# A tiled mixture-of-experts stage: first weights from memory for each tile, and the sums of seven batches on VectorE

## The reference

```python
# B, T, C = 8, 512, 128; 16 heads of 64; E = 8 experts, K = 2, I = 512
x = layernorm(x + attention(x))                # q, k with rope, causal softmax, out @ Wo + bo
weights = softmax(x @ gate_w.T + expert_bias)
top_w, top_i = top_k(weights, 2)
top_w = top_w / (sum(top_w) + 1e-6)
for e in range(E):
    h = gelu(x @ w_up[e].T)                    # 128 -> 512
    out += sparse_w[..., e] * (h @ w_down[e].T)   # 512 -> 128
out = (out - mean(out)) * rsqrt(var(out) + 1e-5) + x
x = layernorm(x + out)
```

## Time and profile before

| | before |
|---|---|
| three runs, us | 857.59, 857.94, 859.91 (median 857.94) |
| profiled execution, us | 857.98, its span 856.2 |
| PE busy | 809.1 us, 95% of the span |
| VectorE, ScalarE, GpSimd busy | 679.8, 630.8, 560.5 us |
| chain that ended last | PE 88%, DVE 5%, ACT 2%, POOL 2% |
| granted PE clock, mean | 0.984 |
| transfers | 41.43 MB, mean 48 GB/s |

### The profile page before, as it was taken

How to read it: one execution, slowest core, us unless ns; L and a number is a source line. 1 busy time by engine, 2 the same in 40 slices (tenths; PEclk the granted TensorE clock), 3 DMA queues, 4 the chain that set the end, 5 groups by cost and what they waited for, 6 DMA issues and landing times.

```text
span 856.2 us, 20971 instructions
## 1 busy us (share of the span) xinstructions
PE 809.1 (95%) x6238; PEld 582.7 (68%) x6238; DVE 679.8 (79%) x2696; ACT 630.8 (74%) x1674; POOL 560.5 (65%) x587
## 2 busy tenths in 40 slices
PE   7999999999999999999999999999999899999950
PEld 2556666666666666666666666666666599999950
DVE  5777798889888988898888889888988576333695
ACT  3677887888788778877787788777787856556543
POOL 4665656556755665576668665765686178898982
PEclk9999999999999999999999999999999999999985
DMA  5111101001000100010001000100022232322714
GB/s 160 32 39 38 51 20 32 8 23 37 28 26 17 48 17 27 14 51 14 26 14 51 14 28 17 48 14 17 28 60 70 67 91 73 79 76 83 212 65 123
DMA packets 52414, 41.43 MB, mean 48 GB/s; under 512 B 6096, under 2 KB 46160, under 8 KB 52304
## 3 DMA queue, kind: packets, MB, share of 16 engines
q1 hardware_dynamic: 47952, 31.11, 13.2%
q0 software_dynamic: 4352, 8.99, 3.0%
HBM read 23.74 MB, written 12.14 MB: 42 GB/s over the span
## 4 chain that ended last, share of the span: by engine, by line
PE 88%; DVE 5%; ACT 2%; POOL 2%; issue 2%; DMA 0%; POOLq 0%; SPq 0%; DVEq 0%; ACTq 0%
PE TB L864 18%; PE SB L824 17%; PE TB L850 14%; PE AO L885 6%; PE SB L997 6%; PE AO L745 4%; PE SB L850 3%; PE AO L747 3%; PE AO L746 3%; PE AO L1006 3%; PE TB L1006 3%; PE AO L742 1%; PE AO L813 1%; PE AO L815 1%; PE AO L814 1%
## 5 line engine op out<-in xcount | busy, mean ns | idle before, releaser
L1083 ACT ACTIVATE Pr_all<-Sm,nmax 128x512 f32<-128x512 f32 (+3 forms) x512 | 279.6, 550 | 2.3 <-DVE nmax L1259 2.3
L1259 DVE CUSTOM_DVE_ANT_0 Sm<-SB,causal 128x512 f32<-128x512 f32 (+3 forms) x512 | 220.0, 486 | 72.2 <-PE SB L824 72.2
L534 POOL TENSOR_TENSOR shared<-shared,sin_t 128x512 f32<-128x512 f32 x63 | 80.3, 1274 | 187.0 <-DVE shared L1239 187.0
L1095 ACT ACTIVATE PT<-TB 128x1024 f32<-128x1024 f32 (+1 forms) x188 | 133.0, 742 | 65.4 <-PE TB L850 65.4
L824 PE MATMUL SB<-kT,qT 64*128 64x512 f32 (+3 forms) x1024 | 167.0, 444 | 2.4 <-DVE nmax L1259 1.9
L864 PE MATMUL TB<-PT,shared 128*64 128x128 f32 x1008 | 152.1, 441 | 2.4 <-ACT PT L1095 0.5
L1280 DVE SCALAR_TENSOR_TENSOR x_acc<-AO,rinv,x_acc 128x128 f32<-128x128 f32 x504 | 141.7, 344 | 5.1 <-PE AO L885 2.8
L850 PE MATMUL TB<-ident,Pr_all 128*128 128x128 f32 x1008 | 134.7, 277 | 1.6 <-ACT PT L1095 1.6
L850 PEld LDWEIGHTS TB<-ident,Pr_all 128*128 128x128 f32 x1008 | 108.6, 140 | 38.8 <-ACT Pr_all L1083 20.6
L824 PEld LDWEIGHTS SB<-kT,qT 64*128 64x128 f32 x1024 | 78.8, 187 | 72.0 <-issue 52.3
L1083 ACT ACTIVATION_READ_ACCUMULATOR Pr_all<-Sm,nmax 128x1 f32 x512 | 97.1, 190 | 0.0
(11 more groups left out here) (281 smaller groups left out, 1425.7 us busy)
## 6 DMA issues: line engine op xcount, KB each, us to landing
wo<-in_wo SPq DMA_DIRECT2D x64, 64.0 KB, 1.8
PT<-yrows SPq DMA_DIRECT2D x7, 512.0 KB, 4.7
xt<-xrows SPq DMA_DIRECT2D x40, 65.0 KB, 2.1
x_acc<-in_x SPq DMA_DIRECT2D x8, 256.0 KB
wdown<-in_wdown SPq DMA_DIRECT2D x8, 256.0 KB, 3.3
pay<-pay SPq DMA_DIRECT2D x8, 256.0 KB, 2.8
x_acc<-pay SPq DMA_DIRECT2D x8, 256.0 KB, 3.2
shared<-in_wup SPq DMA_DIRECT2D x8, 256.0 KB, 3.0
```

The costliest lines, as they stand in the source:

```text
L534: nc.gpsimd.tensor_tensor(k_rot, k_rot, sin_t[:, :], ALU.mult).then_inc(k_mul, 1)
L1083: nc.scalar.activation(Pr[j][:, 0:n], Sm[j], ACT.Exp, bias=nmax[:, j:j + 1], scale=-1.0, accum_out=rsum[p][:, h * QB + qb:h * QB + qb + 1] ...
L1095: last = nc.scalar.activation(PT[p][:, :, 0:qb + 1, qb * P:qb * P + P], source, ACT.Copy)
L1259: nc.vector.tensor_tensor_reduce(out=Sm[j], in0=SB[2 * (group % 2) + h][:, at:at + n], in1=causal[:, T - n:T], scale=-0.125, scalar=HUGE, ...
```

## The change

First weights are no longer kept on chip: SP loads the 256 KB of the tile's expert from memory into `w_tile[t % 4]`, four steps after the tile's rows (`XLEAD`). VectorE copies nothing between tiles, runs batch 7's routing without waiting for tiles, and then sums and measures batches 0 to 6 in two groups and one (`settle`, `root_front`). GpSimd's sums are gone; its spacers end at tile 66. There are 71 tiles. The batch loads and the pads move: pads to SP's steps 24 to 31, batch loads behind the weights of tiles 56 to 59, 64 and 65. ScalarE's order in the tail follows. The core of the diff:

```diff
-TILES = (B * T * K + E * (P - 1)) // P + 1
-TILES += -TILES % 4
+TILES = (B * T * K + E * (P - 1)) // P
+TABLE = TILES + -TILES % 4
-UP_AT = {58: (4,), 59: (5,), 60: (0, 1), 61: (2, 3), 62: (6, 7)}
-LAST_COPY, LAST_BEFORE = 20, (5, 6, 9, 11)
-LAST_PADS = (25, 26, 27, 28, 29, 30, 31, 32)
-LOAD_AT = {0: 63, 1: 64, 2: 65, 3: 66, 4: 71, 5: 71}
-POOL_SUM_AT = {56: (3, 0), 57: (3, 2), 61: (4, 0), 62: (4, 2), 63: (5, 0), 64: (5, 2)}
-AHEAD = GROUP
+LAST_COPY, LAST_BEFORE = 14, (5, 6, 9, 11)
+LAST_PADS = (24, 25, 26, 27, 28, 29, 30, 31)
+LOAD_AT = {0: 56, 1: 57, 2: 58, 3: 59, 4: 64, 5: 65}
+AHEAD, XLEAD = GROUP, 4
...
         @block.sync
-                if u in UP_AT:
...
-            def load_up(e):
-                sp.dma_start(wup[:, e * I:e * I + I], wup_h[:, e * I:e * I + I]).then_inc(w_in, 16)
...
-            def tile_loads(t, s, first, last):
+            def load_rows(t, s):
...
+            def load_weights(t):
+                if t == 2:
+                    sp.wait_ge(scored, BLK * (UNITS - 1))
+                if t % GROUP == 0:
+                    experts[:] = values(mybir.EngineType.SP, tile_expert, t, GROUP, E - 1)
+                wait(sp, up_done, t - AHEAD + 1)
+                sp.dma_start(w_tile[t % AHEAD][:, :], wup_h[:, bass.ds(experts[t % GROUP] * I, I)]).then_inc(w_tile_in[t % AHEAD], 16)
+            rows, experts = [None] * GROUP, [None] * GROUP
+            for t in range(TILES + XLEAD):
+                if t == EARLY:
+                    last_rows()
+                if t < TILES:
+                    load_rows(t, t % XT)
+                if t >= XLEAD:
+                    load_weights(t - XLEAD)
                 for b, at in LOAD_AT.items():
-                    if t == at:
+                    if t - XLEAD == at:
                         load_y(b)
...
         @block.gpsimd
-                if t in POOL_SUM_AT:
-                    sum_half(*POOL_SUM_AT[t])
-                elif t < TILES - 2:
+                if t < TILES - 4:
                     space()
...
         @block.tensor
-                pe.wait_ge(w_ready, t + 1)
+                pe.wait_ge(w_tile_in[t % AHEAD], 16 * (t // AHEAD + 1))
...
-                    pe.wait_ge(w_in, 16 * 2 * E)
+                    pe.wait_ge(w_in, 16 * E)
...
         @block.scalar
             root_half(0, FRONT)
-            root_sum(FRONT, KNOWN + 1)
             for b in range(FRONT):
                 norm2_of(b, QB - 1, 1)
             root_half(FRONT, KNOWN)
+            for b in range(FRONT, KNOWN):
+                norm2_of(b, QB - 1, 2)
+            root_half(KNOWN, KNOWN + 1)
             root_sum(B - 1, B)
-            norm2_of(FRONT, QB - 1, 2)
-            root_half(KNOWN, KNOWN + 1)
-            norm2_of(FRONT + 1, QB - 1, 2)
...
         @block.vector
-            def take_expert(t, e):
-                wait(dve, up_done, t - AHEAD + 1)
-                nc.vector.tensor_copy(w_tile[t % AHEAD][:, :], wup[:, bass.ds(e * I, I)]).then_inc(w_ready, 1)
...
+            def root_front(first, end):
+                of = slice(QB * first, QB * end)
+                bits, root, old = row_bits[:, 0:QB * (end - first)], rstd2[:, 0, of], root_f[:, 0:QB * (end - first)]
+                dve.wait_ge(var1, end)
...
+                for i in range(NEWTON):
...
-            tiles(dve, ffn)
+            for t in range(LAST_TABLE + 9):
+                route_last(t)
...
+            def settle(first, end):
+                for b in range(first, end):
+                    sum_two(b, b)
+                    stats_sum(b)
+                root_front(first, end)
+                for b in range(first, end):
+                    add_x1(b)
+                    stats_half(b)
+            settle(0, FRONT)
+            settle(FRONT, KNOWN)
+            sum_two(KNOWN, KNOWN)
+            stats_sum(KNOWN)
+            factors(1, 0, FRONT)
+            root_front(KNOWN, KNOWN + 1)
+            factors(2, FRONT, KNOWN)
+            add_x1(KNOWN)
+            stats_half(KNOWN)
+            factors(3, KNOWN, KNOWN + 1)
             sum_last()
-            stats_half(KNOWN)
-            factors(2, FRONT, KNOWN)
-            invert_sum(2, B - 1, B)
+            invert_sum(1, B - 1, B)
             add_x1(B - 1)
-            factors(3, KNOWN, KNOWN + 1)
             stats_half(B - 1)
             factors(4, B - 1, B)
```

More of the change, by code:

```diff
@@ L286, in build_block @@
         up_done, gelu_done = sem("up_done"), sem("gelu_done")
-        w_ready = sem("w_ready")
+        w_tile_in = [sem(f"w_tile_in{i}") for i in range(AHEAD)]
         down_done, y_ready = sem("down_done"), sem("y_ready")
@@ L475, in tile_loads @@
                 sp.dma_start(xt[s], xrows[bass.ds(rows[t % GROUP], P), :]).then_inc(xt_in[s], 16)
+            def load_weights(t):
[13 more added lines that the diff above has]
+                    load_weights(t - XLEAD)
                 for b, at in LOAD_AT.items():
-                    if t == at:
+                    if t - XLEAD == at:
                         load_y(b)
-            rows = [None] * GROUP
-            tiles(sp, tile_loads, last_rows)
             for b in range(KNOWN, B):
@@ L1502, in final_table @@
                 if step == 8:
[L1503 removed]
+                    write_tables(1, route_bank(B - 1), slice(EARLY, TABLE))
             def attention(u, p, n, batch, first, last):
@@ L1606, in route_last @@
                     final_table(t - LAST_TABLE)
-                for b in range(FRONT):
-                    if t == SUM_AT.get(b):
-                        sum_two(b, b)
-                    if t == STATS2_AT[b]:
-                        stats_sum(b)
-                if t == ROOT_AT:
-                    seed_front()
-                if t == ROOT_REST_AT:
-                    refine_front(2)
-                for b in range(FRONT):
-                    if t == ADD_AT[b]:
-                        add_x1(b)
-                    if t == HALF_AT[b]:
-                        stats_half(b)
             def norm_rows(b):
@@ L1650, in refine_front @@
-            def refine_front(n):
-                for i in range(n):
-                    root = rstd2[:, 0, front]
-                    done(nc.vector.tensor_tensor(root_f[:, :], root, root, ALU.mult))
-                    done(nc.vector.scalar_tensor_tensor(out=root_f[:, :], in0=root_f[:, :], scalar=-0.5, in1=sd2[:, 0, front],
-                                                        op0=ALU.mult, op1=ALU.mult))
-                    done(nc.vector.scalar_tensor_tensor(out=root, in0=root_f[:, :], scalar=1.5, in1=root, op0=ALU.add, op1=ALU.mult))
@@ L1659, in ffn @@
-            def ffn(t, s, first, last):
-                if first:
-                    dve.wait_ge(tables_ready, 1)
-                    dve.wait_ge(w_in, 16 * 2 * E)
-                    for ahead, e in enumerate(experts(0, AHEAD)):
-                        take_expert(ahead, e)
-                if t == EARLY - AHEAD:
-                    dve.wait_ge(tables_ready, 2)
-                if t in EXPERTS_AT:
-                    of = EXPERTS_AT[t]
-                    next_experts.extend(experts(of[0], of[1] - of[0]))
-                if t + AHEAD < TILES:
-                    take_expert(t + AHEAD, next_experts[t])
-                route_last(t)
+            def root_front(first, end):
+                of = slice(QB * first, QB * end)
+                bits, root, old = row_bits[:, 0:QB * (end - first)], rstd2[:, 0, of], root_f[:, 0:QB * (end - first)]
+                dve.wait_ge(var1, end)
+                done(nc.vector.tensor_scalar(sd2[:, 0, of], mv2[:, 0, of, 1], 4.0, 4 * LN_EPS, ALU.mult, ALU.add))
+                done(nc.vector.tensor_scalar(bits, sd2[:, 0, of].bitcast(I32), 1, None, ALU.arith_shift_right))
+                done(nc.vector.tensor_scalar(root.bitcast(I32), bits, -1.0, ROOT_SEED, ALU.mult, ALU.add))
+                for i in range(NEWTON):
+                    done(nc.vector.tensor_tensor(old, root, root, ALU.mult))
+                    done(nc.vector.scalar_tensor_tensor(out=old, in0=old, scalar=-0.5, in1=sd2[:, 0, of], op0=ALU.mult, op1=ALU.mult))
+                    done(nc.vector.scalar_tensor_tensor(out=root, in0=old, scalar=1.5, in1=root, op0=ALU.add, op1=ALU.mult))
```

52 lines of the change are left out of this document (3 added, 49 removed).

## The result

The changed kernel takes 864.21 us (median of 5 runs, 863.23 to 865.39) beside 859.91 for the kernel before in the same session (5 runs, 857.59 to 860.78): a ratio of 1.0058, 95% interval 1.0039 to 1.0078. It is slower by 0.6%. The forecast was 859.7 against 857.94; by the ratio the result is 862.9 on that footing (857.94 x 1.0058), inside the range and 3.2 us above the sum.

What follows compares the result with a forecast made beforehand. It took PE, without idle time over the tiles, and then a tail of normalisation to bound the kernel. Terms -1.9 + 5.4 + 2.5 - 4.3 = +1.7 us on 857.94 gave 859.7, range 853.5 to 867.5.

Steps and rivals of the forecast that it cites:

- SP's queue at the pads: At tiles 20, 24 and 28, table reads and pads delay SP's weight loads; PE waits 0.8, 3.3 and 1.3: together 5.4 us.
- The batch loads, 2.5 predicted: After tiles 56 to 59, 512 KB loads make SP's steps 2.05 us: weights 2.3 late, tile 66's 0.2; together 2.5 us.
- Landing: ... 3.2: Each 256 KB weight load lands 3.2 us after issue: 3.0 plus 0.2 for the rows queued ahead.
- 0.4 late within those 2.3: Behind the batch loads, 2.6 us of transfer work in 2.05 us steps makes tile 59's weights 0.4 late, inside the 2.3.
- The tail, -4.3 predicted: From the last result to the last normalisation: 18.5 us in place of 22.8, VectorE later than ScalarE by 0.3.
- one tile fewer, -1.9: On PE's path: 71 tiles instead of 72 save one beat, 1.9 us.
- SP keeps up: Rival: reads overlap or SP's steps are cheaper, stalls are 0, VectorE sets the tail: 852.6 us; chance 0.2, wholly or mostly.
- Landings late everywhere: Rival: weight loads take 5.0 us, eleven groups lose 0.6 each, bad places 1.8 more: +8.4, 868.1 us; chance 0.2.
- PE's clock: Rival: PE's clock falls in longer stalls, each tile after costing up to 1.9 us more; counted within late landings' 0.2.
- a stall of 3.3 us: PE's predicted wait before tile 24; shorter than 4.2 us of idle time, so the clock stays at 2.4 GHz.
- the forecast's own range, 857 to 863: Whole kernel: spread of the main forecast, by table reads of 1.3 or 1.5 us and landings of 2.8 to 3.8.
- line of 0.3%: Whole kernel: smallest difference a measurement can tell, 2.6 us; chances faster 0.22, same 0.41, slower 0.37.

Runs made afterwards that it cites:

- fixed_experts: The changed kernel with SP reading no table of experts, tile t taking expert t modulo 8: 859.7 us, 1.0006 of the kernel before.
- pads_spread: The changed kernel with pads sent at SP's steps 25, 27, 29 to 39 instead of 24 to 31: 865.39 us, 1.0089 of the kernel before.
- deep8: The changed kernel with eight buffers for the first weights instead of four: 861.6 us, 1.0039 of the kernel before.
- pool_reads: The changed kernel with GpSimd adding two SBUF buffers of 448 columns behind each send from tile 58 on: 884.24 us, 1.0271 of the kernel before.
- tiles71: The kernel before with 71 tiles instead of 72, the loads of batches 4 and 5 one step earlier: 857.51 us, 0.9991 of the kernel before.
- deep8_spaced: The changed kernel with eight weight buffers and the loads of batches 0 to 5 three tiles apart: 872.33 us, 1.0134 of the kernel before.
- half_weights: The changed kernel with each tile's weight load bringing 128 KB instead of 256 KB: 864.04 us, 1.0068 of the kernel before.

## Why the prediction came out as it did

*SP's queue at the pads, 5.4 predicted.* Right, 6.1: SP's times to 0.3 us, and the cause (`fixed_experts`, `pads_spread`, `deep8`). At tile 28 PE was 5.1 us behind the kernel before (tile 0's 0.4 taken off), where 5.4 was predicted; part of it had come out early, at tiles 21, 25 and 26, whose loads took 3.9 to 4.7 us and not 3.2. The other 0.9, at tile 29, is a landing of 4.9 and was not predicted.

*The batch loads, 2.5 predicted.* **This is the step that was wrong in size**, 5.9. "Landing: ... 3.2" was taken for every load, alone or behind 512 KB. The transfers' side was in the text: 2.6 us of work in steps of 2.05, and it said "0.4 late within those 2.3". But work that isn't done stays in the queue for the next step, so by the prediction's own figures four steps leave 2.2 us; and if loads are served in order, an estimate, a weight load issued 1.15 us behind a batch load that takes 4.7 alone can't land before 3.6 us. Measured, from the issue of the weights of tiles 57 and 58 on: 4.8 and 6.7, where 3.9 and 4.7 were to spare. By place: up to tile 60 PE lost 3.6 us, 2.3 predicted, mostly at 57 and 58, while the prediction had put the loss at 60 and let a lateness at 59 of 0.4 be part of it; at tiles 65 and 66 it lost 2.1, 0.2 predicted. With halved batch loads it is 2.2 up to tile 60, the wait at tile 53 included, which is the predicted term, and still 1.5 at 65 and 66.

*The tail, -4.3 predicted.* -4.8, and the parts: VectorE and ScalarE level, twelve normalisations in one run, additions at 1.11 (`pool_reads`). That the two were level is partly luck: both came about 4.1 us later than predicted, ScalarE for PE's waits, VectorE because it could begin batch 3 only 2.4 later (batch 2's data had come at 806.7) and its two groups of root steps took 3.3 and 2.9 us instead of 2.4 each. One thing was said wrongly about it: it was added to "one tile fewer, -1.9" and to PE's stalls as if PE's last result set the end on both sides. In the kernel before VectorE did, by 6 us (`tiles71` gains 0.8, not 1.9). What the change does is to make VectorE's part overlap PE's longer stay; without PE's waits VectorE is the next limit: `fixed_experts` wins 5.7 us at the last result and 3.9 at the last normalisation.

*Rivals.* SP keeps up: no, PE loses 6.1 to its queue at the pads. Landings late everywhere: no, no tile from 30 to 56 waits for weights. PE's clock: 1.00 through the changed kernel's longest wait of 2.0, but the reason given for it, that a stall of 3.3 us is short enough, does not hold. The clock fell to 0.50 after waits of 2.0 (`deep8`), 2.1 and 2.5 (`deep8_spaced`) and 2.9 (`pads_spread`), and stayed at 1.00 after 2.4 (`half_weights`), 2.6 and 3.0 (`pool_reads`). Had tile 24's wait been the 3.3 that was predicted, the rows don't say which it would have been.

*The range and the chances.* The range of 14 us was wide for the sake of two rivals, and neither came true; the forecast's own range, 857 to 863, holds 862.9 by the ratio and not the measured 864.2. By the prediction's own line of 0.3% the result is "slower" (its interval begins at 0.39%), which had 0.37 against 0.41 for "same". So the direction and three of the terms were understood, and that the time fell inside is owed in part to room left for other causes.

## What to carry to other kernels

A queue that feeds the critical engine has a throughput as well as a lead: SP needed 7.1 of 7.6 us a group (tile 28's weights to tile 32's), so the pads' work, in both placings and with four or eight buffers, came out at PE for the most part. Price a transfer by what is queued ahead of it, carried from step to step, not by its landing alone. And before counting a gain at the last result, ask which engine sets the tail.

## What the runs showed of the hardware

- SP reads a table at 0.33 to 0.36 us a value: 1.34 to 1.43 for four, 2.6 to 2.75 for eight.
- The transfer engines moved 381 to 387 GB/s at a share of 1.03 to 1.08 in the changed kernel's fullest stretches of 2 us, and at most 399 in any kernel here (`pads_spread`). In a burst, one load of 256 KB came after 3.0 us and a later one after 4.9.
- VectorE's additions of two inputs in SBUF, 1.11 us a batch, took 3.41 beside two GpSimd additions of 1.15, and 1.10 to 1.14 beside GpSimd's writes of 0.49.
- After 4.0 to 5.9 us without work PE's granted clock was 0.50 (1.2 GHz), with products of 2.07 to 2.08 in place of 1.06. After waits of 2.0 to 3.0 us it fell in four cases and stayed at 1.00 in others, so the length of the last wait alone does not tell.
- GpSimd's sends one after another every 1.26 us, without the writes between, went with a standstill of VectorE for 9.4 us, of ScalarE for 6.3 and of PE for 4.6; the cause is open.
